# Mixing and splitting of the filter weights moved from a stage of its own into the first normalisation

## What is computed

```python
def _layernorm(x, axis=-1, eps=1e-5):
    m = jnp.mean(x, axis=axis, keepdims=True)
    v = jnp.var(x, axis=axis, keepdims=True)
    return (x - m) / jnp.sqrt(v + eps)
...
        red = jnp.einsum('bchw,oc->bohw', x, w_reduce) + b_reduce[None, :, None, None]
...
            s = sigma ** SIGMA_POW
            out = jnp.einsum('btkd,k,kde->bte', U_plus, s, Mpp)
            out = out + jnp.einsum('btkd,k,kde->bte', U_minus, s, Mpm)
```

## Time and profile before

| | us |
|---|---|
| median of 3 runs | 3113.92 |
| the three runs | 3119.89, 3101.46, 3113.92 |
| the profiled execution | 3099.33 |
| its span in the trace | 3097.6 |
| first instruction of `normalise_in` in the trace | 84.76 |
| first instruction of `involution` in the trace | 243.27 |

### The profile page before, as it was taken

One profiled execution on the slowest core, in us unless ns is written; L12 is line 12 of the kernel. 1 busy time (PEld: TensorE's weight loads), 2 busy tenths in 40 slices (PEclk: granted clock), 3 DMA queues, 4 the chain that ended last, 5 costly groups with the idle time before them and its releaser, 6 DMA issues. The chain is left out here.

```text
span 3097.6 us, 87088 instructions
## 1 busy us (share of the span) xinstructions
PE 2450.0 (79%) x36136; PEld 1874.9 (61%) x36136; DVE 1541.0 (50%) x3563; ACT 1359.1 (44%) x2720; POOL 314.7 (10%) x607
## 2 busy tenths in 40 slices
PE   0455998544609999998999898999979697599998
PEld 0334888522208888888888887888843463144444
DVE  6441343333505656465555555656621165277777
ACT  0562344255006556565656565656621076133332
POOL 0102111100020000000000000000012100122221
PEclk9765899777859999999999999999989698699999
DMA  6437555432461111111111111111048740000000
GB/s 200 128 97 122 104 104 104 118 120 106 139 135 34 43 41 42 42 42 42 42 42 42 42 42 40 44 37 47 22 145 294 260 128 15 12 23 22 23 22 28
DMA packets 189077, 242.74 MB, mean 78 GB/s; under 512 B 36891, under 2 KB 147278, under 8 KB 185146
## 3 DMA queue, kind: packets, MB, share of 16 engines
q1 hardware_dynamic: 154325, 124.05, 15.0%
q0 software_dynamic: 30368, 94.52, 11.3%
q10 hardware_dynamic: 3969, 18.31, 1.5%
HBM read 145.54 MB, written 91.27 MB: 76 GB/s over the span
## 5 line engine op out<-in xcount | busy, mean ns | idle before, releaser
L958 DVE COPY spc_g<-spc_pz 128x512 f32<-128x512 f32 x1088 | 670.4, 683 | 457.3 <-PE spc_pz L856 457.1
L936 ACT ACTIVATE spc_g<-spc_pz 128x512 f32<-128x512 f32 x1088 | 587.6, 610 | 353.4 <-PE spc_pz L856 351.2
L856 PE MATMUL spc_pz<-spc_v,spc_as 108*128 108x128 bf16 x8704 | 604.5, 223 | 46.8 <-issue 32.9
L856 PEld LDWEIGHTS spc_pz<-spc_v,spc_as 108*128 108x128 bf16 x8704 | 519.8, 99 | 141.6 <-issue 51.7
L874 PE MATMUL spc_pz<-spc_g,spc_u 128*20 128x128 f32 x17408 | 499.6, 274 | 27.8 <-DVE spc_g L958 18.3
L874 PEld LDWEIGHTS spc_pz<-spc_g,spc_u 128*20 128x20 f32 x17408 | 479.7, 133 | 56.9 <-ACT spc_g L936 41.3
L841 PE MATMUL spc_pu<-spc_f,spc_s 128*128 128x256 f32 x816 | 223.7, 400 | 71.8 <-DMA spc_s<-s_sf 71.8
L1470 PE MATMUL moe_ex<-moe_ew,moe_d 128*128 128x512 f32 x512 | 249.8, 610 | 33.0 <-DVE moe_yt L1627 32.6
L1627 DVE SCALAR_TENSOR_TENSOR moe_yt<-moe_ex,moe_gb,moe_yt 128x128 f32<-128x128 f32 x768 | 209.6, 344 | 103.3 <-ACT moe_yt L1529 101.0
L505 DVE SCALAR_TENSOR_TENSOR inv_xo<-inv_pa,inv_mask,inv_xo 128x256 f32<-128x256 f32 x256 | 123.6, 484 | 222.3 <-PE inv_pa L463 161.2
L483 ACT ACTIVATE inv_b<-inv_pb 112x1024 f32<-112x1024 f32 x128 | 125.1, 1021 | 222.0 <-PE inv_pb L442 222.0
(11 more groups left out here) (199 smaller groups left out, 2214.7 us busy)
## 6 DMA issues: line engine op xcount, KB each, us to landing
s_yd<-spc_yo SPq DMA_DIRECT2D x136, 160.0 KB
spc_s<-s_sf POOLq DMA_DIRECT2D x36, 512.0 KB, 6.6
ivs_y<-s_yd POOLq DMA_DIRECT2D x34, 512.0 KB, 5.1
s_td<-ivs_to SPq DMA_DIRECT2D x34, 512.0 KB, 4.7
s_sf<-fwd_so ACTq DMA_DIRECT2D x16, 1024.0 KB, 4.7
ln_t<-s_td SPq DMA_DIRECT2D x32, 512.0 KB, 3.7
inv_x<-s_xn SPq DMA_DIRECT2D x88, 112.0 KB
inv_x<-s_xn POOLq DMA_DIRECT2D x88, 112.0 KB, 8.0
```

Source lines behind the costliest of these rows:

```text
L856: m = pe.matmul(pz[:, (p + 2) % 3, e // 4, 2 * FT * (e % 4):2 * FT * (e % 4) + 2 * FT], AS[:, x, 8 * p + e, :], V[:, k, x, :, FT * t:FT * ...
L936: act.activation(g_out(p, 0), g_in(p, 0), ACT.Copy).then_inc(ga, 1)
L958: v.tensor_copy(g_out(p, 1), g_in(p, 1)).then_inc(gd, 1)
```

## The change

The stage `prepare` is dropped and its buffers, loads, stores and computations are put into `normalise_in`. Nothing of the computation is changed, and none of the rounds' own instructions.

- SP: the three constants of the normalisation come first, then the five small tensors, experts 0 and 1, all ten zero writes, and then the stores of the rounds. Behind the first stored tile of round 1 (q == 4) expert 2 is loaded, behind the last of round 1 (q == 7) expert 3, followed by `D2M`; the first parts are stored behind the second tile of round 4 (q == 17), the others behind the second tile of round 6 (q == 25).
- ScalarE: the exp and the two square roots come ahead of the rounds.
- VectorE: memset and the argument of the exp come ahead of the rounds. In round i, between the computation of -mean/sd (L341 of the kernel before) and the addition of the bias (L349), stands `weights(i)`: the mixture and expert 0 in round 0, expert 1 in round 1, experts 2 and 3 in round 2, the first combination and its split in round 3, the second combination in round 4, its split in round 5. Rounds 6 and 7 have none.

The diff, cut to its core:

```diff
@@ sync
             sp.dma_start(rbias[:], I["b_reduce"]).then_inc(const_in, 16)
+
+            def load_mats(i):
+                for m, name in enumerate(("Mpp", "Mpm")):
+                    sp.dma_start(mp[:, i % 2, m, :].rearrange("e (k d) -> e k d", k=KF),
+                                 I[name][i].rearrange("k e d -> e k d")).then_inc(mats_in[i % 2], 16)
+                sp.dma_start(mu[:, i % 2], I["Mu"][i].rearrange("k e d -> e k d")).then_inc(mats_in[i % 2], 16)
+
+            def store_parts(x):
+                sp.wait_ge(parts_ready, x + 1)
+                for s in range(3):
+                    sp.dma_start(S["AS"][x, s].rearrange("k e d -> e k d"), parts[:, s, :].rearrange(
+                        "e (k d) -> e k d", k=KX)).then_inc(parts_out, 16)
+
...
+            load_mats(0)
+            load_mats(1)
+            sp.wait_ge(zero_ready, 1)
+            for side in (0, HP - PADH):
+                sp.dma_start(S["XN"][side:side + PADH].rearrange("h x y w b c -> (h x y w b c)").rearrange(
+                    "(p m) -> p m", m=2048), zero[0:PADH * HP, :]).then_inc(out_done, 16)
...
             for b in range(NB):
                 for n in range(NCH):
...
+                    if q == D:
+                        sp.wait_ge(mats_used, 1)
+                        load_mats(2)
+                    if q == 2 * D - 1:
+                        sp.wait_ge(mats_used, 2)
+                        load_mats(3)
+                        sp.wait_ge(wc_ready, 1)
+                        sp.dma_start(S["D2M"], d2[:].rearrange("p a b -> p (a b)")).then_inc(out_done, 16)
+                    if q == 4 * D + 1:
+                        store_parts(0)
+                    if q == 6 * D + 1:
+                        store_parts(1)
@@ scalar
             act.wait_ge(eps_ready, 1)
+            act.wait_ge(act_req, 1)
+            act.activation(sm[:, 1, :], sm[:, 0, :], ACT.Exp).then_inc(act_done, 1)
+            act.activation(sg[:, 1, :], sg[:, 0, :], ACT.Sqrt).then_inc(act_done, 1)
+            act.wait_ge(act_done, 2)
+            act.activation(sg[:, 2, :], sg[:, 1, :], ACT.Sqrt).then_inc(act_done, 1)
@@ vector
+            def add_mats(i):
+                v.wait_ge(mats_in[i % 2], 48 * (i // 2 + 1))
...
+            def weights(i):
+                if i == 0:
+                    mixture()
+                    add_mats(0)
+                elif i == 1:
+                    add_mats(1)
+                elif i == 2:
+                    add_mats(2)
+                    add_mats(3)
+                elif i == 3:
+                    combine(0)
+                    split(0)
+                elif i == 4:
+                    combine(1)
+                elif i == 5:
+                    split(1)
...
                     v.scalar_tensor_tensor(nm[:, k], mv[:, k, :, 0], -1.0, rs[:, k],
                                            ALU.mult, ALU.mult).then_inc(nm_ready, 1)
+                weights(i)
                 for k in range(D):
                     b, n = divmod(D * i + k, NCH)
...
-STAGES = (prepare, first_mixer, forward, filters, spectrum, inverse, layer_one)
+STAGES = (first_mixer, forward, filters, spectrum, inverse, layer_one)
```

More of the change, by code:

```diff
@@ L70, in split3 @@
     step(eng.tensor_tensor(lo, tmp, mid, ALU.subtract))
[L73 to L209, removed]
@@ L216, in normalise_in @@
     with Arena(nc, "lnc") as A:
+        lg, sm, s1 = A.sb("lg", [P, 2, 4]), A.sb("sm", [P, 12, 4]), A.sb("s1", [P, 8])
+        prio, sg = A.sb("prio", [P, 4]), A.sb("sg", [P, 3, KF])
+        mp, mu = A.sb("mp", [P, 2, 2, KF * C]), A.sb("mu", [P, 2, 3, C])
+        acc, au = A.sb("acc", [P, 2, KF * C]), A.sb("au", [P, 3, C])
+        ab, tmp = A.sb("ab", [P, KX * C]), A.sb("tmp", [P, KX * C])
+        parts = A.sb("parts", [P, 3, KX * C], BF16)
+        zero = A.sb("zero", [P, 2048])
+        d2, mk = A.sb("d2", [P, 16, 4]), A.sb("mk", [P, 16])
+        small_in, mats_used = A.sem("small_in"), A.sem("mats_used")
+        mats_in = [A.sem(f"mats_in{k}") for k in range(2)]
+        dve_done, act_done, act_req = A.sem("dve_done"), A.sem("act_done"), A.sem("act_req")
+        wc_ready, parts_ready, parts_out = A.sem("wc_ready"), A.sem("parts_ready"), A.sem("parts_out")
+        zero_ready, out_done = A.sem("zero_ready"), A.sem("out_done")
         ident = A.sb("ident", [P, P])
@@ L257, in _ @@
             sp.dma_start(rbias[:], I["b_reduce"]).then_inc(const_in, 16)
+            def load_mats(i):
[8 more added lines that the diff above has]
+                        "e (k d) -> e k d", k=KX)).then_inc(parts_out, 16)
+            sp.dma_start(lg[:, 0, :], I["lw"].partition_broadcast(P)).then_inc(small_in, 16)
+            sp.dma_start(lg[:, 1, :], I["gum"].partition_broadcast(P)).then_inc(small_in, 16)
+            sp.dma_start(sg[:, 0, :], I["sigma"].partition_broadcast(P)).then_inc(small_in, 16)
+            sp.dma_start(prio[:], I["prio"]).then_inc(small_in, 16)
+            sp.dma_start(d2[:], I["d2"].rearrange("p (a b) -> p a b", a=16)).then_inc(small_in, 16)
+            load_mats(0)
[4 more added lines that the diff above has]
+                    "(p m) -> p m", m=2048), zero[0:PADH * HP, :]).then_inc(out_done, 16)
+                sp.dma_start(S["XN"][PADH:PADH + HW, :, :, side:side + PADH].rearrange("h x y w b c -> (h x y) (w b c)"),
+                             zero[:, 0:PADH * NB * C]).then_inc(out_done, 16)
+            for b in range(NB):
+                sp.dma_start(S["SF"][b, 32], zero[:, 0:256]).then_inc(out_done, 16)
+            sp.dma_start(S["SP"][32], zero[:, 0:2 * KX]).then_inc(out_done, 16)
+            sp.dma_start(S["VP"], zero[0:66, 0:NB * 66].rearrange("h (b w) -> h b w", b=NB)).then_inc(out_done, 16)
             for b in range(NB):
@@ L266, in _ @@
                         sp.dma_start(dst.rearrange("u x w c -> (u x) w c"), xn[:, k, t]).then_inc(outs[k], 16)
+                    if q == D:
[10 more added lines that the diff above has]
+                        store_parts(1)
+            sp.wait_ge(parts_out, 96)
+            sp.wait_ge(out_done, 16 * (4 + NB + 3))
             for k in range(D):
@@ L322, in _, with step, mixture @@
         def _(v):
+            steps = [0]
+            def step(ins):
+                steps[0] += 1
+                ins.then_inc(dve_done, 1)
+                v.wait_ge(dve_done, steps[0])
+            def mixture():
+                v.wait_ge(act_done, 3)
+                step(v.tensor_reduce(s1[:, 1:2], sm[:, 1, :], AX.X, ALU.add))
+                step(v.reciprocal(s1[:, 2:3], s1[:, 1:2]))
+                step(v.tensor_scalar(sm[:, 3, :], sm[:, 1, :], s1[:, 2:3], None, ALU.mult))
+                step(v.tensor_reduce(s1[:, 3:4], sm[:, 3, :], AX.X, ALU.max))
+                step(v.tensor_scalar(sm[:, 4, :], sm[:, 3, :], s1[:, 3:4], None, ALU.is_equal))
+                step(v.tensor_tensor(sm[:, 5, :], sm[:, 4, :], prio[:], ALU.mult))
+                step(v.tensor_reduce(s1[:, 4:5], sm[:, 5, :], AX.X, ALU.max))
+                step(v.tensor_scalar(sm[:, 6, :], sm[:, 5, :], s1[:, 4:5], None, ALU.is_equal))
+                step(v.tensor_tensor(sm[:, 7, :], sm[:, 6, :], sm[:, 3, :], ALU.subtract))
+                step(v.tensor_tensor(sm[:, 8, :], sm[:, 7, :], sm[:, 3, :], ALU.add))
+                step(v.memset(mk[:], 0.0))
+                for i in range(4):
+                    step(v.tensor_scalar(mk[:, 0:16 >> i], mk[:, 0:16 >> i], sm[:, 6, i:i + 1], None, ALU.add))
+                v.tensor_tensor(d2[:], d2[:], mk[:].rearrange("p (a o) -> p a o", o=1).to_broadcast([P, 16, 4]),
+                                ALU.mult).then_inc(wc_ready, 1)
@@ new lines, in split @@
+            def split(x):
+                if x:
+                    v.wait_ge(parts_out, 48)
+                split3(v, ab[:], tmp[:], parts[:, 0, :], parts[:, 1, :], parts[:, 2, :], step)
+                v.sem_inc(parts_ready, 1)
+            def weights(i):
+                if i == 0:
+                    mixture()
[12 more added lines that the diff above has]
+                    split(1)
@@ L323, in _ @@
+            v.memset(zero[:], 0.0).then_inc(zero_ready, 1)
+            v.wait_ge(small_in, 16 * 5)
+            step(v.tensor_tensor(sm[:, 2, :], lg[:, 0, :], lg[:, 1, :], ALU.add))
+            step(v.tensor_reduce(s1[:, 0:1], sm[:, 2, :], AX.X, ALU.max))
+            v.tensor_scalar(sm[:, 0, :], sm[:, 2, :], s1[:, 0:1], None, ALU.subtract).then_inc(act_req, 1)
             v.sem_inc(red_ready, 4 * D)
```

14 lines of the change are left out of this document (added).

## The result

The changed kernel took 3063.34 us (median of 4 runs, 3055.94 to 3070.74) against 3107.69 for the kernel before beside it (4 runs, 3098.66 to 3119.89): ratio 0.985 [0.982, 0.988]. Timed side by side again (experiment r1) it was 3077.73 against 3105.20, ratio 0.991 [0.987, 0.994]. Both medians lie in the forecast range of 3034 to 3086; the point of 3065 is 1.7 from the first and 12.7 from the second. The profiled execution took 3063.15 us, its span is 36.3 us shorter than that of before. Runs in the slow state, over 1.5% above the fastest of the same kernel, are left out of ratios and intervals; of those shown this is one, the 3076.66 us of r3.

The account below looks back on a forecast made before the run. Bound: each round's engine chain with 9.15 us of idle VectorE, and the four DMA engines carrying xn stores. Terms -81.4 + 21.8 + 3.3 + 8.2 + 3.7 + 1.5 = -42.9 from 3108.6 gave 3065 us, range 3034 to 3086.

Parts of the forecast that it names:

- start of round 0: Without the first stage, ScalarE's first L313 starts at 15.0 instead of 96.39 us: -81.4 us.
- round 1 waits for the stores of round 0: ScalarE waits for xn stores queued behind experts and zeros on shared DMA engines: +21.8 us.
- round 2 waits for those of round 1: Round 1's later tile stores stand behind expert 2's load in SP's queue, delaying round 2: +3.3 us.
- round 2's piece waits for expert 3: VectorE waits in round 2 for expert 3, landing at 90.0 behind stores, and delays L349: +8.2 us.
- combination and split in round 3: VectorE's 13.1 us of work in round 3 exceeds its 9.15 us of idle time: +3.7 us.
- waits of rounds 4 to 7: The parts' stores in round 4 make tile 3 of round 5 late; nothing in round 6: +1.5 us.
- A: Transfers are hidden: round 0's stores slip past the zeros, expert 3 comes in time; 3032 us, chance 0.10.
- D: Slower than before: SP's one queue becomes the bound and nothing moved is hidden; 3129 us, chance 0.03.
- B: Round 0's stores wait for SP's issuing, not the zeros' engines: 7.4 us less loss, 3058 us, chance 0.23.
- C: Stores beside loads run slower, costing 2.4 us in each of rounds 0 to 5; 3080 us, chance 0.14.
- Waits in rounds 3, 6 and 7: Sign of a wrong forecast: waits for stores in these rounds too; no size given.
- x loads' term: A round's 1.05 MB of x loads takes about 2.4 us on each DMA engine, including the stores' four.

Follow-up runs that it names:

- r3: Changed kernel with late exp and roots, respread VectorE pieces and late zeros from 128 partitions, timed beside the kernel before: median 3046.76 us, ratio 0.980.
- e1: Changed kernel with the two 912 KB zero strips written from 128 partitions instead of 114: next block at 201.23 us instead of 207.05.
- e3: Changed kernel with eight xn buffers instead of four: next block at 208.24 us instead of 207.05.
- e2: Changed kernel with ScalarE's exp and two roots moved behind round 0's four copies: next block at 207.20 us instead of 207.05.
- e7: Changed kernel with late exp and roots, respread VectorE pieces and late zeros from 128 partitions: next block at 185.33 us instead of 207.05.
- e5: Changed kernel with VectorE's pieces spread over rounds 2 to 6 and parts stored behind rounds 4 and 6: next block at 197.23 us instead of 207.05.

## Why the prediction was right, and where it was not

It was right because the losses on the way were found ahead, not only the 81.4 us of the removed stage. In the terms of its sum, with "as if begun" for a broken round meaning its last row's start + 1.65 - 6.27:

| step | forecast | measured |
|---|---|---|
| start of round 0 | -81.4 (at 15.0) | -78.3 (at 18.12) |
| round 1 waits for the stores of round 0 | +21.8 | +20.8 (57.7 for 36.9) |
| round 2 waits for those of round 1 | +3.3 | +3.1 (80.0 for 76.9) |
| round 2's piece waits for expert 3 | +8.2 | +7.9 (26.6 from 80.0 to 106.59, for 18.7) |
| combination and split in round 3 | +3.7 | +3.7 (22.37 for 18.7) |
| waits of rounds 4 to 7 | +1.5 | +5.9 (4.0 in round 5, 1.9 in round 7) |
| rest | 0 | +0.7 |
| sum | -42.9 | -36.2 |

(In the first row 81.4 and 78.3 are counted from 96.39.)

*The bound was named rightly.* The choice between 21.8 (the four engines of the stores lie among the six of the zeros) and 14.4 (they don't) was open in the trace; 20.8 speaks for the first, and the mechanism is shown by the 13.4 us between the last zero write's issue and the first tile's release, and by e1: with the zeros' strips spread wider the stores come 7.5 us earlier, where 7.1 was worked out. So the rule of the Trainium skill ("DMA: Bandwidth & Descriptors", section "Why a DMA increments its semaphore by 16 and not by 1"), that transfers of SP's queue which use few engines all use the lowest ones, agrees with this case's 53.14 and 45.66; it said 21.8 as well. The runs show that stores and zeros share engines, not which numbers these have; that the stores have four is an estimate, for 0.29 of 16 is 4.6. Rivals A and D did not happen. B, of SP's issuing, is refuted: it put the end of the wait at 54, not 62.33, and in e1 the first tile came 7.5 us earlier with the zeros' issuing only 4.2 earlier. C did not happen at its size, for rounds 3, 4 and 6 wait for no store; but what it says, that stores beside loads are slower, is seen in e3.

*The start was mis-sized by 3.1.* Two things were late: VectorE had the small tensors at 8.5 and not at 6.8 (x loads were issued beside them; that these were the cause is argued only), and ScalarE's first table load ran behind its wait, where in the kernel before it had run ahead of all. The first row is of the kernel before, the second of the changed one:

```profile
0.88 1.28 ACT L151 ACT_TABLE_LOAD   x1 [0.88 <-PEq L1760]
9.21 1.28 ACT L219 ACT_TABLE_LOAD   x1 [9.21 <-DVE lnc_sm L316]
```

But e2 shows that the term is worth nothing by itself: round 1 begins when SP's queue lets it. The sum should have had the time of round 1's release (60.3 forecast, 62.3 measured) as one number, and not a gain of 81.4 and a loss of 21.8 which hang on each other.

*Rounds 4 to 7 were mis-sized by 4.4.* For round 5 I set 22.8 us of queue work against 18.7 and took some 3 of slack; the difference is 4.1, and 4.0 was lost. For round 7 I wrote that 20.4 fits in a round of 18.7, which it doesn't by my own numbers: the difference is 1.7, and 1.9 was lost. The bound had been found, and then not been carried through to the end. Waits in rounds 3, 6 and 7 had been named as a sign of being wrong; the one in round 7 came.

*From block to total.* The trace's gain is 36.2 us. The medians differ by 44.4 in the first comparison (3107.69 - 3063.34) and by 27.5 in the second (r1). That 3065 was met to 1.7 us is partly luck: the sum was 6.7 too large, and the runs of that comparison came out about 8 better than the block alone gives. Both are within the spread that the involution's clock makes; whether the changed kernel's later stages are on average any longer or shorter than before stays open, since the kernel before has one trace only.

*The size of the x loads' term.* The 2.4 us a round, on engines that the stores need, was too small where loads and stores ran together: e3 shows 3.6 to 5.0. What this cost in the changed kernel no run separates.

## What to carry to other kernels

Work moved into the idle time of one engine brings its transfers with it. Before counting on cover, sum the work of the busiest DMA engine, not the mean share: a share that stands still at a level such as 0.29 while the engines change their doing says that only four or five of sixteen engines carry that transfer. Look at it by queue, since two queues can add up to such a level, as zeros and x loads did here to 0.37. In e7 such an engine had 183 us to do in a stage whose chain was 162 us. Buffers (e3) and an earlier start (e2) gained nothing; another spread of the pieces (e5) gained 9.8 us, of which 5.9 are the waits of rounds 5 and 7; late zeros from 128 partitions gained 18, and with all three edits another queue for the stores 20 more.

## What was not expected of the hardware

- 114 partitions instead of 128 in two zero writes of 912 KB cost 7.5 us of waiting (53.14 against 45.66).
- Two queues at work together slowed each other, and not evenly: beside the zeros of SP's queue, 64 KB stores from GpSimd's took up to 28.3 us to land, and SP's issuing of one 1 MB load rose from 2.07 to 14.9 us.
- Stores of the same shape had a share of 0.29 and 86 GB/s from SP's queue and 0.49 and 108 GB/s from GpSimd's, each alone.
- The granted clock in one stage differed between runs of the same kernel, 0.84 and 0.76, and with it the stage's length, 362 and 393 us.
